# Second attention with scores in both orientations, the maxima subtracted inside the matmul, and the stacks in four places

## The reference

```
q = rope((x @ Wq) by heads);  k = rope((x @ Wk) by heads);  v = (x @ Wv) by heads
scores = einsum('bhqd,bhkd->bhqk', q, repeat(k, 4)) / 4
attn = softmax(where(key > query, lowest, scores))
ctx = einsum('bhqk,bhkd->bhqd', attn, repeat(v, 4))
x = layernorm(x + ctx.reshape(b, t, 512) @ Wo)
```

## Time and profile before

| | us |
|---|---|
| median of 3 runs | 1177.17 (1176.73 to 1177.77) |
| profiled execution, span from first to last instruction | 1175.2 |
| PE busy in the span | 1135.8 (97%) |
| DVE, ACT, POOL busy | 780.6, 705.3, 410.5 |

### The profile page before, as it was taken

One profiled execution on the slowest core, in us unless ns is written; L12 is line 12 of the kernel. 1 busy time (PEld: TensorE's weight loads), 2 busy tenths in 40 slices (PEclk: granted clock), 3 DMA queues, 4 the chain that ended last, 5 costly groups with the idle time before them and its releaser, 6 DMA issues. The chain is left out here.

```text
span 1175.2 us, 20479 instructions
## 1 busy us (share of the span) xinstructions
PE 1135.8 (97%) x6634; PEld 952.6 (81%) x6634; DVE 780.6 (66%) x2463; ACT 705.3 (60%) x1646; POOL 410.5 (35%) x342
## 2 busy tenths in 40 slices
PE   7899999999999999999999999999999899999997
PEld 6788888788888888888888778888888677777786
DVE  6866776667776667766677762223336899999775
ACT  6656665556665566666566544543112899999524
POOL 4654554255444445534443513334013210020200
PEclk9999999999999999999999999999999999999999
DMA  6011110111110100110100012222001223321001
GB/s 230 19 40 43 37 32 24 30 28 37 53 29 21 37 32 24 55 27 11 45 19 28 1 37 75 68 78 76 1 18 24 57 70 80 98 53 33 2 1 72
DMA packets 30364, 51.24 MB, mean 44 GB/s; under 512 B 5680, under 2 KB 6576, under 8 KB 30256
## 3 DMA queue, kind: packets, MB, share of 16 engines
q1 hardware_dynamic: 29680, 48.85, 14.7%
q10 hardware_dynamic: 576, 1.05, 0.2%
HBM read 38.35 MB, written 2.10 MB: 34 GB/s over the span
## 5 line engine op out<-in xcount | busy, mean ns | idle before, releaser
L487 POOL TENSOR_TENSOR turned<-turned,sin 128x512 f32<-128x512 f32 x73 | 94.4, 1293 | 310.3 <-ACT turned L347 310.3
L363 ACT ACTIVATE probs<-probs,neg_max 128x256 f32<-128x256 f32 (+1 forms) x256 | 119.8, 473 | 11.3 <-DVE neg_max L580 11.3
L1477 ACT ACTIVATE a_probs<-a_probs,a_neg_max 128x512 f32<-128x512 f32 (+3 forms) x256 | 122.6, 562 | 0.1
L1661 DVE CUSTOM_DVE_ANT_0 a_probs<-bank,a_mask 128x512 f32<-128x512 f32 (+3 forms) x256 | 109.8, 486 | 6.2 <-PE bank L1881 6.1
L490 POOL TENSOR_TENSOR turned<-turned,by_cos 128x512 f32<-128x512 f32 x73 | 101.1, 1385 | 5.7
L96 PE MATMUL bank<-wo_hi,oT_hi 128*128 128x512 f32 x256 | 100.3, 392 | 1.7 <-DVE oT_lo L643 1.7
L734 PE MATMUL bank<-xT_hi,wq_hi 128*128 128x512 f32 x256 | 101.7, 397 | 0.0
L734 PE MATMUL bank<-xT_lo,wq_hi 128*128 128x512 f32 x256 | 100.3, 392 | 0.0
L734 PE MATMUL bank<-xT_hi,wq_lo 128*128 128x512 f32 x256 | 100.0, 391 | 0.0
L96 PE MATMUL bank<-wo_hi,oT_lo 128*128 128x512 f32 x256 | 99.9, 390 | 0.0
L96 PE MATMUL bank<-wo_lo,oT_hi 128*128 128x512 f32 x256 | 99.7, 389 | 0.0
(11 more groups left out here) (234 smaller groups left out, 3155.1 us busy)
## 6 DMA issues: line engine op xcount, KB each, us to landing
staged<-weights SPq DMA_DIRECT2D x70, 256.0 KB, 2.7
f_staged<-weights_f SPq DMA_DIRECT2D x33, 256.0 KB, 2.7
a_q_stack<-a_qT_hi SPq DMA_DIRECT2D x64, 64.0 KB, 2.0
rows<-x_rows SPq DMA_DIRECT2D x2, 1024.0 KB, 7.4
a_k_stack<-a_kT_hi SPq DMA_DIRECT2D x64, 32.0 KB, 2.0
a_q_stack<-a_qT_lo SPq DMA_DIRECT2D x32, 64.0 KB, 2.0
out<-rows SPq DMA_DIRECT2D x8, 256.0 KB, 2.0
a_raw<-weights_qkv SPq DMA_DIRECT2D x4, 384.0 KB, 4.4
```

Source lines behind the costliest of these rows:

```text
L363: act.activation(probs[:, s % 2, h, 0:width], probs[:, s % 2, h, 0:width], ACT.Exp, bias=neg_max[:, s % 2, h:h + 1], scale=SCALE0, accum_o ...
L487: pool.tensor_tensor(at, at, sin[:, :], ALU.mult).then_inc(sin_done, 1)
L1477: act.activation(row_probs(s, qt), row_probs(s, qt), ACT.Exp, bias=neg_max[:, h, qt:qt + 1], scale=-1.0).then_inc(exp_done, 1)
L1661: dve.tensor_tensor_reduce(row_probs(s, qt), ps_s[bank][:, at:at + seen], mask[:, SEQ - seen:SEQ], -SCALE1, HIGHEST, ALU.add, ALU.min, neg ...
```

## The change

The scores are computed twice. `scores(s)` and `maxima(s)` stay, but only for the maxima: DVE writes the rest to an unused tile. The maxima of a unit (16 columns of `tops`) are turned by one PE transpose (`turn_tops`), copied and negated by ACT (`copy_tops`) and put by two DMAs of SP (`load_tops`) into rows 96 and 97 of that unit's `q_stack`; `k_stack` has a one there. `key_scores(s)`, four matmuls over 98 rows, then gives scores minus maxima with the keys in rows, ACT takes the exponential straight from PSUM to `pT` in three passes, and POOL clears the masked halves of the four diagonal blocks (`prune`, two instructions a slot). The ten transposes, DVE's and ACT's copies of turned banks and the four wide exponentials are gone. Scores now lead by seven slots, stacks have four places, `pT` eight; `evacuate` is ACT's; the turning of the first four output tiles moves into the last slots, and the last unit's apply behind the first `project_out`. POOL fills the ones of four `k_stack`s during the projections (`pad_keys`).

```diff
+STACKS = 4
+TOP_ROW = STACK
+STACK_ROWS = STACK + 2
+LEAD = 7
+RING, RING_IN_X = 8, 6
...
+            def load_tops(u):
+                sp.wait_ge(top_ready, u + 1)
+                for version in range(2):
+                    rows_of = slice(version * 2 * SEQ_TILES, (version + 1) * 2 * SEQ_TILES)
+                    to = q_stack[u % STACKS][TOP_ROW + version:TOP_ROW + version + 1, :, :].rearrange("a p (t c) -> a (p t) c", c=P)
+                    sp.dma_start(to.bitcast(F32), top_rows[rows_of, :].bitcast(F32)).then_inc(top_in[u % 2], 16)
...
-            for u in range(2, UNITS1):
-                if u == KV1:
-                    sp.wait_ge(part_lo, TURNS_OF[1])
-                sp.wait_ge(scored, PIECES * GROUP1 * (u - 1))
-                load_stacks(u)
+            for u in range(UNITS1):
+                load_tops(u)
+                if u + 2 < UNITS1:
+                    if u + 2 == KV1:
+                        sp.wait_ge(part_lo, TURNS_OF[1])
+                    if u >= 2:
+                        sp.wait_ge(keyed, PIECES * GROUP1 * (u - 1))
+                    load_stacks(u + 2)
...
             def exps(s):
-                h = s % GROUP1
-                for qt in ROW_TILES:
-                    act.wait_ge(max_done, SEQ_TILES * s + maxima_before(qt))
-                    act.activation(row_probs(s, qt), row_probs(s, qt), ACT.Exp, bias=neg_max[:, h, qt:qt + 1],
-                                   scale=-1.0).then_inc(exp_done, 1)
-
-            def copy_turned(s):
                 if s >= RING:
-                    act.wait_ge(applied, 2 * ((s - RING) // GROUP1 + 1))
-                for piece in (1, 2):
-                    width, at = TURNED_WIDTH[piece], piece * SEQ
-                    act.wait_ge(pT_ready, PIECES * s + piece + 1)
-                    act.activation(pT[:, s % RING, at:at + width], ps_t[piece][:, 0:width], ACT.Copy).then_inc(pT_act, 1)
+                    act.wait_ge(applied, APPLY_PARTS * ((s - RING) // GROUP1 + 1))
+                for piece, width in enumerate(KEY_WIDTH):
+                    act.wait_ge(keyed, PIECES * s + piece + 1)
+                    act.activation(pT(s)[:, piece * SEQ:piece * SEQ + width], ps_t[piece][:, 0:width], ACT.Exp,
+                                   scale=SCALE1).then_inc(exp_done, 1)
+
+            def copy_tops(u):
+                act.wait_ge(top_turned, u + 1)
+                act.activation(top_rows[0:4 * SEQ_TILES, :], ps_top[u][0:4 * SEQ_TILES, 0:P], ACT.Copy,
+                               scale=-1.0).then_inc(top_ready, 1)
+
+            def evacuate(n):
+                act.wait_ge(applied, APPLY_PARTS * (n + 1))
+                if n >= 1:
+                    act.wait_ge(o_turned, n)
+                act.activation(oT_now[:, :], ps_o[n % 2][:, :], ACT.Copy).then_inc(o_read, 1)
...
+            copy_values(TILES - 1)
+            act.wait_ge(v_done, TILES)
+            high_part(PARTS_LAST[0])
+            copy_tops(0)
+            high_part(PARTS_LAST[1])
+            high_part(PARTS_LAST[2])
+            for s in range(SLOTS1):
+                exps(s)
+                if s % GROUP1 == 1 and s + 3 < SLOTS1:
+                    copy_tops((s + 3) // GROUP1)
+                if s % GROUP1 == 3 and s >= GROUP1 + 3:
+                    evacuate((s - GROUP1 - 3) // GROUP1)
+                if OUT_AHEAD <= s < OUT_AHEAD + SEQ_TILES:
+                    high_out(s - OUT_AHEAD)
...
+            def pad_keys(n):
+
+                pool.memset(k_stack[n][:, :, :].bitcast(F32), 0.0).then_inc(stack_set, 1)
+                pool.wait_ge(stack_set, 2 * n + 1)
+                pool.affine_select(k_stack[n][:, :, :], k_stack[n][:, :, :], [[-1, 2], [0, SEQ]], ALU.not_equal, 1.0,
+                                   base=-TOP_ROW, channel_multiplier=1).then_inc(stack_set, 1)
+
...
+            def prune(s):
+
+                pool.wait_ge(exp_done, PIECES * (s + 1))
+                for first, step in ((0, SEQ), (SEQ + 3 * P, P)):
+                    pair = pT(s)[:, first:first + 2 * step].rearrange("p (a c) -> p a c", a=2)[:, :, 0:P]
+                    pool.affine_select(pair, pair, [[0, 2], [1, P]], ALU.is_ge, 0.0, base=0,
+                                       channel_multiplier=-1).then_inc(pruned, 1)
+
...
                     bank, at = SCORES_AT[qt]
                     seen = (qt + 1) * P
                     dve.wait_ge(scored, PIECES * s + bank + 1)
-                    dve.tensor_tensor_reduce(row_probs(s, qt), ps_s[bank][:, at:at + seen], mask[:, SEQ - seen:SEQ],
-                                             -SCALE1, HIGHEST, ALU.add, ALU.min,
-                                             neg_max[:, s % GROUP1, qt:qt + 1]).then_inc(max_done, 1)
-
...
+                    dve.tensor_tensor_reduce(unused[:, UNUSED_AT[qt]:UNUSED_AT[qt] + seen], ps_s[bank][:, at:at + seen], mask[:, SEQ - seen:SEQ],
+                                             1.0, LOWEST, ALU.add, ALU.max, top_column(s, qt)).then_inc(max_done, 1)
...
+            maxima(2)
+            maxima(3)
+            low_part(PARTS_LAST[0])
+            maxima(4)
+            low_part(PARTS_LAST[1])
+            maxima(5)
+            low_part(PARTS_LAST[2])
+            maxima(6)
...
+            for s in range(SLOTS1):
+                if s % GROUP1 == 1 and s >= 2 * GROUP1 + 1:
+                    join((s - 2 * GROUP1 - 1) // GROUP1)
+                if s + LEAD < SLOTS1:
+                    maxima(s + LEAD)
+                if OUT_AHEAD <= s < OUT_AHEAD + SEQ_TILES:
+                    low_out(s - OUT_AHEAD)
...
+            def key_scores(s, piece):
+
+                u, h = divmod(s, GROUP1)
+                if h == 0 and piece == 0:
+                    pe.wait_ge(top_in[u % 2], 32 * (u // 2 + 1))
+                if s >= 1:
+                    pe.wait_ge(exp_done, PIECES * (s - 1) + piece + 1)
+                for kb in KEY_PIECES[piece]:
+                    at = KEYS_AT[kb][1]
+                    mm = pe.matmul(ps_t[piece][:, at:at + SEQ - kb * P],
+                                   k_stack[u % STACKS][0:STACK_ROWS, h % 2, kb * P:(kb + 1) * P],
+                                   q_stack[u % STACKS][0:STACK_ROWS, h // 2, kb * P:SEQ], start=True, stop=True,
+                                   skip_group_check=True)
+                mm.then_inc(keyed, 1)
...
+            def turn_tops(u):
+                pe.wait_ge(max_done, SEQ_TILES * GROUP1 * (u + 1))
...
+                pe.transpose(ps_top[u][:, 0:P], tops[:, u % 2, :], ident[:, :]).then_inc(top_turned, 1)
...
-            for s in range(SLOTS1 + 2):
-                if s < SLOTS1:
-                    turn(s)
-                if s >= GROUP1 and s % GROUP1 < 2:
-                    apply(s // GROUP1 - 1, s % GROUP1)
-                if s == 0:
-                    scores(2)
-                if s % GROUP1 == 3 and s >= GROUP1:
-                    turn_output(s // GROUP1 - 1)
-                if s + AHEAD_SCORES < SLOTS1:
-                    scores(s + AHEAD_SCORES)
-                if s in PARTS_IN_LOOP:
...
+            def lead(s):
+                for piece in range(PIECES):
+                    scores(s, piece)
+
+            lead(2)
+            lead(3)
+            turn_part(PARTS_LAST[0])
+            lead(4)
+            turn_tops(0)
+            turn_part(PARTS_LAST[1])
+            lead(5)
+            turn_part(PARTS_LAST[2])
+            lead(6)
...
+            for s in range(SLOTS1):
+                if s + LEAD < SLOTS1:
+                    lead(s + LEAD)
+                for piece in range(PIECES):
+                    key_scores(s, piece)
+                if s % GROUP1 == 1 and s + 3 < SLOTS1:
+                    turn_tops((s + 3) // GROUP1)
+                if s >= APPLY_LAG and (s - APPLY_LAG) % GROUP1 < APPLY_PARTS:
+                    apply((s - APPLY_LAG) // GROUP1, (s - APPLY_LAG) % GROUP1)
+                if s % GROUP1 == 0 and s >= 2 * GROUP1:
+                    turn_output(s // GROUP1 - 2)
+                if s == OUT_AHEAD:
+                    pe.wait_ge(max_done, SEQ_TILES * SLOTS1)
+                if OUT_AHEAD <= s < OUT_AHEAD + SEQ_TILES:
+                    turn_out(s - OUT_AHEAD)
...
             for tile in range(TILES):
                 project_out(tile)
+                if tile == 0:
+                    turn_output(UNITS1 - 2)
+                    for part in range(APPLY_PARTS):
+                        apply(UNITS1 - 1, part)
+                if tile == 1:
+                    turn_output(UNITS1 - 1)```

On PE, at the change of units. Before, a slot of the loop is scores of slot s+3, ten transposes of slot s+1, and here the apply of the unit before (bank numbers and stack places are shown):

```order
L1881 MATMUL bank0<-a1_k_stack,a1_q_stack 128x512 [waits a1_max_done,a1_stack_in0]
L1881 MATMUL bank1<-a1_k_stack,a1_q_stack 128x384 [waits a1_max_done]
L1881 MATMUL bank1<-a1_k_stack,a1_q_stack 128x128
L1881 MATMUL bank2<-a1_k_stack,a1_q_stack 128x256 [waits a1_max_done]
```

(32 more changed lines are left out.)

208 lines of the change are left out of this document (89 added, 119 removed).

## The result

| | us |
|---|---|
| before, median of 4 runs | 1176.95 (1176.66 to 1177.77) |
| after, median of 4 runs | 1214.94 (1213.90 to 1216.14) |
| ratio after / before, 95% interval | 1.0319 (1.0304 to 1.0333) |
| profiled execution of after, span | 1214.3 (before 1175.2) |

Slower by 38 us; forecast 1202, range 1191 to 1220. The page of the changed kernel: PE and the granted clock in 40 slices, and the chain that ended last by engine.

A forecast was written before the change was run, and what follows sets the result against it. Before, PE, ACT and DVE were within 4%; after, a 13.0 us ring through SP, PE and ACT binds. Wo starts 21.3 us later, plus 3.4 behind it: 1199.9 span, plus 2.0 gives 1202 us, range 1191 to 1220.

The forecast's parts named there:

- the ring: SP's stack DMAs wait for ACT's maxima copy, which needs PE past the stack before: 13.0 us a unit; chance 0.60.
- The start: Before the rounds: SP starts at 918.55, unit 2's stack is in at 928.7 and the scores of slot 8 begin.
- The rounds: From the scores of slot 8 to those of slot 60: 13 rounds of 13.0 us, ending at 1097.7.
- the issuing: SP's 14 DMAs a unit, issued one after the other: 13 steps of 0.625 us, 8.13 us.
- the exponentials: ACT's three exponentials a slot out of PSUM, inside the round: 1.36 us.
- the second rival: PE idles about 3.5 us a unit, so its clock may fall to half: some 0.75 us a round, 1212 us; chance 0.20.
- From slot 60 to Wo: No stack left to load, PE runs freely to the first product with Wo: 22.0 us, starting at 1119.7.
- Behind it: In the stage with Wo, the last apply and two output turns are added on PE: 3.4 us.
- The weak step: PE's idle 3.5 us a unit lies nearer to a 2.7 us wait at full clock than to 6.54 at half.
- Its 1212: Total in us if every unit's PE work behind the DMA wait pays for half clock, by the skill's rule.
- What would show it: Signs: 13 or 14 PE waits of about 3.5 us at L1926, 14 SP DMAs in a row, PE some 70% busy.
- POOL and the pads: Select taken at 0.6 us, POOL setting the unit above 1.62, chance 0.04; pads costed at nothing, 3 us for the upper end.

The follow-up runs named there:

- e9: The changed kernel with 17 products of 128x512 added on PE ahead of its wait for each new stack, from unit 6 on: 1214.66 us.
- the last run: The changed kernel with ACT issuing the maxima's DMAs, 24 products between scores of slots 2 to 6 and ten ahead of the last turning of parts: 1150.84 us.
- e7: The changed kernel with ten products of 128x512 added on PE ahead of its wait for each new stack, from unit 6 on: 1214.49 us.
- e10: The changed kernel with 17 products of 128x512 added on PE ahead of its wait for each new stack, from unit 7 on: 1210.69 us.

## Why the prediction was right, step by step

**The mechanism** was the forecast one: the ring, at the place and with the length worked out. It is shown by four edits that open or shorten it (SP's order, ACT's queue, PE's order, four DMAs) and leave the arithmetic as it is.

**Where the 14.4 us between the forecast span (1199.9) and the measured one (1214.3) lie:**
- The start: scores of slot 8 at 929.52 against 928.7, 0.8 us.
- The rounds: 1108.60 - 929.52 = 179.1 us for 13, 13.78 each against 13.0, so 10.1 us. In a round whose scores ran at full clock (13.10 to 13.19) the mis-sized term is the issuing, 8.34 to 8.42 us for 8.13, mostly since the two new DMAs take 0.69 us apiece and not 0.625; the exponentials, 1.24 for 1.36, give half of it back. That is 0.15 a round, 2 us. The largest part is the half clock, 0.84 in the seven rounds that began at it, 5.9 us. The other 2.2 lie in the two rounds by the loads of w_o and in two with a stretched issue (14.58, 13.42). The half clock was the second rival, priced at 0.75 a round and given 0.20; it came true in seven of 13 rounds and should have had a larger chance.
- From slot 60 to Wo: 25.8 against 22.0. The 17 products in the wait (e9) cut this by 2.6 (23.2 us from the scores of slot 60, at 1109.91, to Wo), which is the clock; the other 1.2 us were counted too low.
- Behind it: 79.9 us against 76.8 in before, 3.1, forecast 3.4.

**The weak step** is the one on the clock. I read from the earlier trace rows that a wait of 2.7 us left the clock at full and 6.5 did not, and placed 3.5 by distance. But the length of a wait does not tell. The wait of the earlier trace rows is in the profile of after too, 2.73 us long, and there the clock fell behind it. The wait is 2.72 to 2.75 us long in all twelve profiles; in ten the clock fell in it or right behind it, and before, from which I read, is one of the two where it did not: bad luck. The wait in after, and the same stretch of time in after and then in before (the clock is the third number from the end):

```profile
47.91 0.66 PE L773 MATMUL bank<-identity,probs 128*128 128x128 f32 x4 [2.73 <-DVE probs L592]
```
```profile
49.31:52.72 3.41, 3.25 (x11) 2.34 (x10) 3.37 (x12) 0.63 (x1) 1.38 (x1) 0.50 0.22 65
```
```profile
49.31:52.72 3.41, 2.03 (x13) 1.47 (x12) 3.38 (x12) 0.63 (x1) 1.44 (x1) 1.00 0.22 70
```

In the slots, eight of the 13 waits, of 1.40 to 3.96 us, ended at half clock, five, of 2.15 to 2.59, at full. Behind these five the clock fell as well, but only 1.25 to 1.9 us after the wait's end, and the four scores and the first key score that the ring needs of PE take 1.23. The half clock, over 3 us each time, then met work on which the ring does not wait. The first and the last of the five:

```profile
1014.04:1015.27 1.23, 1.23 (x8) 1.14 (x8) 0.70 (x3) 0.00 (x0) 0.00 (x0) 1.00 0.00 0
1015.30:1018.70 3.40, 3.40 (x21) 1.35 (x20) 1.01 (x6) 1.46 (x4) 0.77 (x2) 0.50 0.02 6
...
1095.47:1097.20 1.73, 1.73 (x13) 1.49 (x17) 1.19 (x5) 0.50 (x2) 0.00 (x0) 1.00 0.00 0
1097.25:1100.60 3.35, 3.35 (x21) 1.69 (x14) 1.01 (x5) 0.94 (x4) 1.19 (x3) 0.50 0.01 2
```

The one unit without a wait, unit 6 at 986.91 us, kept full clock up to the next wait. So each wait had a stretch of half clock with it, and what decided over the round was where that stretch began. By the rule of the Trainium skill (TensorE: Matmul & The Clock Gate, section "HAM oscillation — how this bites in real kernels") every unit would pay. The trace agrees for PE's work behind all 13 waits, and for the length of the round in seven. Its 1212 was nearer to 1214.9 than the forecast.

**What would show it**, point by point: 13 waits at L1926 for `q_stack`, forecast 13 or 14, but of 2.5 us and not 3.5, since half clock stretches PE's work from 8.8 to 10.6 us and more. 14 DMAs in a row and then ACT's copy, as said. PE's busy share in the rounds 81% (10.6 of 13.1) where some 70% was forecast, for the same reason.

**POOL and the pads** were rightly put aside. The select is as cheap as the lower bound, 0.40 us:

```profile
L1659 POOL TENSOR_SCALAR_AFFINE_SELECT f_pT<-f_pT 128x256 f32<-128x256 f32 x96 | 36.7, 406 | 110.8 <-ACT f_pT L1511 110.8
```

The wait for w_o held POOL for 6.6 us, not 4, and the two units beside it were 14.4 and 14.3 us, 0.4 over the half-clock rounds. The pads did not delay the start: SP's first stack issue is at 900.0 in both.

## What to carry to other kernels

Follow each wait on a DMA queue back to what releases it, and ask whether that needs something that stands behind the same queue: here two new DMAs in front of twelve old ones closed a loop of SP, PE and ACT that no engine's busy time shows, and turned 21 us of gain into 38 of loss. Four buffers do not help when the transfer that fills the next one is queued behind a result of the last. The edit that opens it is one of order, or a second queue for the small, late transfers.

## What the runs showed of the hardware

- The granted clock stayed at 0.5 for 17.6 and 19.8 us of PE work without a gap (the two windows above), while at the program's start the matmuls were at full speed after some 6 us, and behind five waits in after the clock was back at 1.0 within 3.5 us. Work without a gap did not always bring it back soon.
- Small gaps stood ahead of a fall: waits of 1.87 and 1.85 us at the start of the slots, and one of 0.51 us in the last run, with PE busy 13.2 of 13.9 us. That these gaps are the cause is argued, not shown; filling the first two moved the fall behind them.
- The same wait of 2.72 to 2.75 us in the first attention had a fall of the clock with it in ten of twelve profiles, in two none.
- Ten products in the wait did not hold the clock in every unit, seventeen did (mean clock 1.00 over 107 us).
- Issuing a DMA costs ACT about what it costs SP: the two of the maxima took 1.31 us on ACT and 1.38 on SP.
- Of the fourteen issues of a unit one at times took 1.2 to 1.7 us in place of 0.59, with products in the wait and without (after, e7, e10); the cause was not looked for.
